# Layer 2's experts in an order by places, and layer 3's attention prepared beside their last two chunks

## What is computed

```python
h = _layernorm(x, axis=-1) * (1 + cb) + sb                      # layer 2
x = x + gb * _L2_ffn_ref(h, ...)
...
h = _layernorm(x, axis=-1) * (1 + ca) + sa                      # layer 3
x = x + ga * _L3_attn_ref(h, W_qkv, b_qkv, W_out, b_out)
h = _layernorm(x, axis=-1) * (1 + cb) + sb
x = x + gb * _L3_ffn_ref(h, ...)

def _L2_ffn_ref(x, ...):
    weights, idx = _gate(xf, gate_w, gate_b)
    combine = (one_hot(idx, E) * weights[..., None]).sum(1)
    h = silu(xf @ We1 + be1) * (xf @ We3 + be3)
    y = einsum('te,ted->td', combine, h @ We2 + be2)
    z = (silu(xf @ ws1 + bs1) * (xf @ ws3 + bs3)) @ ws2 + bs2
    return y + z

def _L3_attn_ref(x, W_qkv, b_qkv, W_out, b_out):
    T, B, D = x.shape
    q, k, v = split(x @ W_qkv + b_qkv)
    scores = einsum('bhqd,bhkd->bhqk', q, k) / sqrt(Dh)
    attn = softmax(where(causal, scores, -inf))
    return (attn @ v) @ W_out + b_out
```

## Time and profile before

| | us |
|---|---|
| median of 3 runs | 3118.23 |
| lowest and highest run | 3110.52 and 3121.22 |
| the profiled execution, device time | 3117.64 |
| its span | 3115.7 |
| PE busy | 2809.0 (90%) |
| DVE busy | 2174.2 (70%) |
| ACT busy | 1692.5 (54%) |
| POOL busy | 1048.9 (34%) |

### The profile page before, as it was taken

One profiled execution on the slowest core, in us unless ns is written; L12 is line 12 of the kernel. 1 busy time (PEld: TensorE's weight loads), 2 busy tenths in 40 slices (PEclk: granted clock), 3 DMA queues, 4 the chain that ended last, 5 costly groups with the idle time before them and its releaser, 6 DMA issues.

```text
span 3115.7 us, 68897 instructions
## 1 busy us (share of the span) xinstructions
PE 2809.0 (90%) x25404; PEld 1878.9 (60%) x25404; DVE 2174.2 (70%) x5846; ACT 1692.5 (54%) x4067; POOL 1048.9 (34%) x1444
## 2 busy tenths in 40 slices
PE   5999999989999999999997998999899889885885
PEld 2566666666666666666665554677666655554664
DVE  5888888855666466666666888556677868864557
ACT  2877777773233377777764666433255442223553
POOL 5877788731000011111113444222433300114323
PEclk8999999999999999999998999999899999897997
DMA  3011111122000011111114443000344422335640
GB/s 101 15 29 29 29 29 29 29 82 84 15 1 1 19 29 29 29 29 29 29 29 138 125 130 109 1 15 1 102 139 121 118 62 56 70 71 151 169 118 28
DMA packets 189836, 188.13 MB, mean 60 GB/s; under 512 B 14288, under 2 KB 166032, under 8 KB 188736
## 3 DMA queue, kind: packets, MB, share of 16 engines
q1 hardware_dynamic: 189504, 183.73, 22.5%
HBM read 130.36 MB, written 53.31 MB: 59 GB/s over the span
## 4 chain that ended last, share of the span: by engine, by line
PE 61%; DVE 21%; issue 6%; ACT 6%; POOL 2%; DMA 2%; SPq 2%; DVEq 0%; POOLq 0%; ACTq 0%
PE pb L174 55%; ACT big L895 4%; PE pb L620 2%; DVE big L2107 2%; DVE big L785 2%; DVE big L240 2%; SPq L1788 2%; DVE big L768 1%; ACT big L171 1%; DVE big L696 1%; DMA big<-parts 1%; DVE big L2579 1%; DVE big L190 1%; DVE big L767 1%; PE pb L553 1%
## 5 line engine op out<-in xcount | busy, mean ns | idle before, releaser
L174 PE MATMUL pb<-big 128*128 128x128 f32 (+13 forms) x20220 | 2528.5, 332 | 186.8 <-DVE big L2107 58.9
L174 PEld LDWEIGHTS pb<-big 128*128 128x128 f32 (+5 forms) x20220 | 1572.0, 146 | 942.5 <-issue 545.8
L171 ACT ACTIVATE big<-pb 128x512 f32<-128x512 f32 (+7 forms) x1444 | 826.1, 619 | 594.6 <-PE pb L174 348.0
L171 ACT ACTIVATE big<-pb,big 128x512 f32<-128x512 f32 (+2 forms) x504 | 308.7, 632 | 677.3 <-PE pb L174 542.1
L2107 DVE TENSOR_REDUCE big<-pb 128x4 f32<-128x1024 f32 (+1 forms) x256 | 278.2, 1087 | 111.6 <-PE pb L174 108.2
L185 POOL TENSOR_TENSOR big<-big 128x128 f32<-128x128 f32 x224 | 99.9, 461 | 748.8 <-DVE big L182 748.8
L895 ACT ACTIVATE big<-big 128x256 f32<-128x256 f32 x512 | 253.9, 497 | 71.0 <-DVE big L790 69.4
L895 ACT ACTIVATE big<-pb,big 128x128 f32<-128x128 f32 (+1 forms) x512 | 255.6, 513 | 64.6 <-DVE big L770 64.1
L974 POOL TENSOR_TENSOR big<-big 128x512 f32<-128x512 f32 x128 | 159.7, 1274 | 247.6 <-DMA big<-recip 247.6
L785 DVE CUSTOM_DVE_ANT_0 big<-pb,big 128x256 f32<-128x256 f32 x512 | 186.6, 421 | 78.4 <-PE pb L174 78.2
L1470 DVE SCALAR_TENSOR_TENSOR big<-pb,big 128x128 f32<-128x128 f32 x512 | 144.0, 344 | 139.1 <-PE pb L174 138.5
(11 more groups left out here) (136 smaller groups left out, 2321.2 us busy)
## 6 DMA issues: line engine op xcount, KB each, us to landing
big<-parts SPq DMA_DIRECT2D x96, 512.0 KB, 4.1
parts<-big SPq DMA_DIRECT2D x384, 96.0 KB, 2.3
big<-recip SPq DMA_DIRECT2D x64, 512.0 KB, 6.7
big<-comb SPq DMA_DIRECT2D x32, 512.0 KB, 8.4
parts<-big SPq DMA_DIRECT2D x192, 64.0 KB, 2.1
big<-gates SPq DMA_DIRECT2D x8, 1024.0 KB, 6.1
big<-in_wa SPq DMA_DIRECT2D x2, 2048.0 KB, 9.0
big<-in_wf SPq DMA_DIRECT2D x1, 3072.0 KB, 14.8
```

The source lines that it names most:

```text
L171: return e.activation(o, i, f, bias=bias, scale=scale)
L174: return e.matmul(o, l, r_, start=start, stop=stop, skip_group_check=True)
```

## The change

- The experts of layer 2 take their tiles by `by_places`: chunk c holds the tiles `8 * (c % 4) + 2 * i + c // 4`, so chunks 0 to 3 are the first half of the places of all batches, and chunks 4 to 7 the second. The modulated copy of a chunk is made by four activations of 128 columns instead of two of 256.
- Layer 3's attention gives a guest of 15 steps, and the experts host it from tick 54 (chunk 6) to tick 68. Steps 0 to 9 hold statistics, norms and turns of its chunks 0 to 3, steps 10 to 14 `qk`, `split` and `v` of groups 0 to 2. SP issues `out` 0, `back` 0, `out` 1, `back` 1 and `out` 2 at the end of the experts' own DMAs; `back` 1 waits until `summed` is 64, that is for the matmuls of tick 63 (`tensor_down`), since its target is memory that the experts still read.
- The fence between the two stages goes. PE waits for the experts' PSUM banks before the loop, and for chunk 7's multiplies at tick 3.
- The gates and weights for the last stage are loaded behind group 6's parts instead of ahead of all.
- Of the eight chunks of results that are added to `X` four, the first half of the places, are transposed and added in ticks 46, 49, 52 and 55 (`y_at`), with banks of the loop's ring; four stay behind the loop.

```diff
@@ -199,14 +199,19 @@
+        def by_places(c):
+            return [8 * (c % 4) + 2 * i + c // 4 for i in range(4)]
         chunks = [0]
...
-            def __init__(self, own_v, own_g, mod, which, slots, r0, two_slots=False, tiles=None):
+            def __init__(self, own_v, own_g, mod, which, slots, r0, two_slots=False, tiles=None, same_order=False):
+                self.ready = (lambda c: 4 * c + 4) if same_order else (lambda c: max(self.tiles(c)) + 1)
                 self.tiles = tiles or (lambda c: range(4 * c, 4 * c + 4))
@@ -222,7 +227,7 @@
                 elif i0 == 0:
-                    e.wait_ge(added, self.r0 - 32 + max(self.tiles(c)) + 1)
+                    e.wait_ge(added, self.r0 - 32 + self.ready(c))
                 stats_vector(e, self.ov, [X[:, self.tiles(c)[i], :] for i in range(i0, i1)], self.slot(c) + i0, mean_made if i1 == 4 else None)
@@ -269,8 +274,10 @@
                 for i, tile in enumerate(self.tiles(c)):
-                    b, d = tile // 2, dst(tile)
-                    src = s.t[:, 128 * i:128 * i + 128].rearrange("p (i t) -> p i t", i=d.shape[1])
+                    b, d = tile // 2, dst(i)
+                    src = s.t[:, 128 * i:128 * i + 128]
+                    if len(d.shape) == 3:
+                        src = src.rearrange("p (i t) -> p i t", i=d.shape[1])
                     t = act(e, d, src, ACT.Identity, self.mod[:, self.which, b:b + 1], self.mod[:, self.which + 1, b:b + 1])
@@ -1186,8 +1193,9 @@
             modulated_at = 3 * nunit + (0, 2, 1)[k]
-            guests_at = 7 * nunit
-            norm = Norm(own, own_g, MODS[k % 2], 2, slots, r0) if X1 is None else None
+            guests_at = (6 if pairs else 7) * nunit
+            tiles = by_places if pairs else lambda c: range(4 * c, 4 * c + 4)
+            norm = Norm(own, own_g, MODS[k % 2], 2, slots, r0, tiles=tiles) if X1 is None else None
@@ -1456,7 +1464,7 @@
                             n = r0 + 4 * c + i
-                            residual_vector(e, n, 4 * c + i, banks[4 + c % 2][:, 128 * i:128 * i + 128], 128).then_inc(gated, 1)
+                            residual_vector(e, n, tiles(c)[i], banks[4 + c % 2][:, 128 * i:128 * i + 128], 128).then_inc(gated, 1)
                     return
...
@@ -1541,7 +1549,9 @@
                         start.ht_free(e)
-                    if p == "turn":
+                    if p == "turn" and pairs:
+                        norm.modulated_tiles(e, c, lambda n: HTS[s][:, 128 * n:128 * n + 128])
+                    elif p == "turn":
                         norm.modulated(e, c, lambda n: HTS[s][:, 256 * n:256 * n + 256])
...
@@ -1699,7 +1709,13 @@
                 guest.ht_free = ht_free
-                guest.mem_free = nothing
+                def mem_free(e):
+                    if pairs:
+                        s = slots["v", 6 * nunit + 7, 0]
+                        e.wait_ge(s.free, s.n)
+                guest.mem_free = mem_free
             yield Stage(tensor, vector, scalar, gpsimd, sync)
@@ -2402,7 +2418,7 @@
             OV = [alloc(512) for _ in range(2)]
-            bqs = alloc(1)
+            bqs = bqs1
             bias_scaled, q_out = sem("bias_scaled3"), sem("q_out3")
@@ -2413,10 +2429,10 @@
             parts = Parts(own_g, p0, 4, wait_qk)
-            ring = BK[5:8]
+            ring = [BK[6], BK[7], BK[5]]
             taken = [0]
             slots = {}
-            norm = Norm(own, own_g, MODS[1], 0, slots, residuals[0], two_slots=True, tiles=lambda c: [8 * (c % 4) + 2 * i + c // 4 for i in range(4)])
+            norm = Norm(own, own_g, MODS[1], 0, slots, residuals[0], two_slots=True, tiles=by_places, same_order=True)
@@ -2427,7 +2443,12 @@
-            prologue = [(g, p) for g in range(3) for p in ("qk", "split", "v") if p != "v" or g < 2]
+            def hosted_step(i):
+                found = [(c, p) for c in range(4) for p, at in (("stats", 0), ("normed", 1), ("ln", 3)) if 2 * c + at == i]
+                return found + {10: [(0, "qk"), (0, "split")], 11: [(0, "v")], 12: [(1, "qk"), (1, "split")], 13: [(1, "v")],
+                                14: [(2, "qk"), (2, "split")]}.get(i, [])
@@ -2438,9 +2459,13 @@
-            def take(*key):
-                slots[key] = ring[taken[0] % 3].use()
+            def take(*key, ring=ring):
+                slots[key] = ring[taken[0] % len(ring)].use()
                 taken[0] += 1
+            def y_at(t):
+                return [(t - 46) // 3] if t >= 46 and (t - 46) % 3 == 0 and (t - 46) // 3 < 4 else []
@@ -2523,13 +2548,26 @@
+            def tensor_hosted(e, i):
+                if i == 0:
+                    e.wait_ge(ld_wi, 48)
+                for g, p in hosted_step(i):
+                    tensor_piece(e, g, p)
+            def tensor_y(e, c):
+                s, v = slots["y", c], slots["c", 16 * (c // 4) + 15]
+                e.wait_ge(v.free, v.n)
+                bk = fill(e, s)
+                for i, ti in enumerate(by_places(c)):
+                    x = e.transpose(bk[:, 128 * i:128 * i + 128], YT[:, ti // 2, 128 * (ti % 2):128 * (ti % 2) + 128], IDF)
+                x.then_inc(s.full, 1)
             def tensor(e):
-                e.wait_ge(ld_wi, 48)
-                for c in range(4):
-                    norm.turn(e, c)
-                for g, p in prologue:
-                    tensor_piece(e, g, p)
+                for bank, n in settled:
+                    e.wait_ge(bank.free, n)
                 for t in range(last):
+                    if t == 3:
+                        e.wait_ge(gated, 96)
                     if t < 64:
@@ -2559,15 +2597,10 @@
                         tensor_piece(e, g, p)
-                s = slots["c", 31]
-                e.wait_ge(s.free, s.n)
-                for c in range(8):
-                    s = slots["y", c]
-                    bk = fill(e, s)
-                    for i in range(4):
-                        ti = 4 * c + i
-                        x = e.transpose(bk[:, 128 * i:128 * i + 128], YT[:, ti // 2, 128 * (ti % 2):128 * (ti % 2) + 128], IDF)
-                    x.then_inc(s.full, 1)
+                    for c in y_at(t):
+                        tensor_y(e, c)
+                for c in range(4, 8):
+                    tensor_y(e, c)
@@ -2614,18 +2647,22 @@
+            def vector_hosted(e, i):
+                if i == 0:
+                    e.wait_ge(ld_wi, 48)
+                    e.tensor_scalar(bqs, bi[:, 0:1], 8.0 ** -0.5, None, ALU.mult).then_inc(bias_scaled, 1)
+                    ones_vector(e)
+                for g, p in hosted_step(i):
+                    vector_piece(e, g, p)
+            def vector_y(e, c):
+                s = slots["y", c]
+                bk = empty(e, s)
+                xs = X[:, 8 * (c % 4):8 * (c % 4) + 8, :].rearrange("p (i h) c -> p i h c", h=2)[:, :, c // 4, :]
+                e.tensor_tensor(xs, xs, bk[:, :].rearrange("p (i c) -> p i c", i=4), ALU.add).then_inc(s.free, 1)
             def vector(e):
-                e.wait_ge(ld_wi, 48)
-                e.tensor_scalar(bqs, bi[:, 0:1], 8.0 ** -0.5, None, ALU.mult).then_inc(bias_scaled, 1)
-                ones_vector(e)
                 pads_vector(e, True)
-                norm.stats(e, 0)
-                for c in range(4):
-                    if c < 3:
-                        norm.stats(e, c + 1)
-                    norm.normed(e, c)
-                for g, p in prologue:
-                    vector_piece(e, g, p)
                 for t in range(last):
...
@@ -2654,12 +2690,14 @@
+            def scalar_hosted(e, i):
+                for g, p in hosted_step(i):
+                    if g == 0 and p == "qk":
+                        start.mem_free(e)
+                        e.wait_ge(bias_scaled, 1)
+                    scalar_piece(e, g, p)
             def scalar(e):
-                for c in range(4):
-                    turned_back(e, c)
-                e.wait_ge(bias_scaled, 1)
-                for g, p in prologue:
-                    scalar_piece(e, g, p)
                 for t in range(last):
...
@@ -2715,23 +2753,29 @@
-            def sync(e):
-                second_gates(e, 3)
-                e.dma_start(WF[:, 0:dr["wf3"].shape[1]], dr["wf3"]).then_inc(ld_wf, 16)
+            def sync_hosted(e):
                 parts.out(e, 0)
...
                 parts.out(e, 1)
-                for g in range(2, 16):
+                e.wait_ge(summed, 64)
+                parts.back(e, 1)
+                parts.out(e, 2)
+            def sync(e):
+                for g in range(3, 16):
                     parts.out(e, g)
                     parts.back(e, g - 1)
+                    if g == 6:
+                        e.wait_ge(gated, 96)
+                        second_gates(e, 3)
+                        e.dma_start(WF[:, 0:dr["wf3"].shape[1]], dr["wf3"]).then_inc(ld_wf, 16)
                 parts.back(e, 15)
-            yield None, None
-            for c in range(4):
-                take("ln", c)
```

(10 more changed lines are left out.)

26 lines of the change are left out of this document (13 added, 13 removed).

## The result

| | before | changed |
|---|---|---|
| median, lowest and highest run, us | 3119.72 (3110.52 to 3124.09, 4 runs) | 3087.56 (3077.55 to 3088.29, 4 runs) |
| the profiled execution, us | 3117.64 | 3088.29 |

The ratio is 0.9893, with a 95% interval of 0.9863 to 0.9924: faster by 1.1%, and 4.6 us over the predicted 3083. Measured a second time beside other kernels, with four runs of it, the ratio was 0.9889 (0.9874 to 0.9904), the median 3084.63. Of `back_at_once`, `back1_behind_out2`, `host_later` and `host_earlier` there is one run each (3086.70, 3084.12, 3091.88 and 3095.59 us), so they are read by marks inside their profiles and not by whole times.

A forecast was written before the change was run, and what follows sets the result against it. TensorE bounds the experts' last chunks, then 37.9 us lie before layer 3's first maximum, with a second hole before tick 4. Summed: -36.0 at tick 8, +0.8 early results, +0.5 gates, -34.7 from 3117.64, so 3083 us; range 3074 to 3099.

The forecast's parts named there:

- order of the places: Experts' chunks of layer 2: four smaller ACT activations a chunk are hidden, cost nothing; 6 us in all without that cover.
- hosted work beside the experts: Experts' chunks 6 and 7: layer 3's hosted preparation makes the experts end 7.5 us later, ends 5 and 12.
- tick 8, hosting included: Layer 3's loop: tick 8's maximum comes 36.0 us earlier, after a new wait of 2.3 us for back 2.
- gates and weights at group 6: Loop at group 6: two SP issues and data sharing the DMA engines cost 0.5 us, ends 0 and 4.
- early results in the loop: Loop ticks 46, 49, 52, 55: four adds cost 3.2 us together, 1.1 each at 46 and 52.
- four adds fewer in the tail: Tail behind the loop: four of DVE's eight transposed chunks leave, 2.4 us less.
- PE work alone: Low end for hosting in chunks 6 and 7: only PE's added turns, qk and v count, 5 us.
- Start of the loop: First score maximum of layer 3: at 2804.9 instead of 2833.40, 28.5 us earlier.
- a granted clock of 1.00 from the experts on through the loop: Sign expected in the changed kernel: PE keeps its full 2.4 GHz clock from the experts on through layer 3's loop.
- Rival A: Loop: the sync queue sets the pace with slow issues, tick 8 some 3 us later, +11 us, 3094; chance 0.15.
- Rival B: Beside the experts: VectorE and GpSimd hold each other up, norms 6.4 us dearer, experts and copies 8 later, 3091; chance 0.10.
- Rival C: Experts' last chunks: PE waits in order for hosted work, 26 us and up to 39, so 3148, slower; chance 0.03.

The follow-up runs named there:

- back_at_once: Changed kernel, but from group 2 on SP issues a group's copies back right behind its own copies out; 3086.70 us, one run.
- back1_behind_out2: Changed kernel with group 2's copies out issued ahead of group 1's copies back, SP's old order for that step; 3084.12 us, one run.
- host_later: Changed kernel with its 15 hosted steps at ticks 57 to 71 instead of 54 to 68; 3091.88 us, one run.
- host_earlier: Changed kernel with its 15 hosted steps at ticks 51 to 65 instead of 54 to 68; 3095.59 us, one run.
- order_alone: Kernel before with only the new order of the places, nothing hosted and no result added sooner; ratio 1.0004 to the kernel before.
- results_in_tail: Changed kernel with all eight results added in the tail, none in the loop; median 3080.06 us, ratio 0.988 to the kernel before.
- again_before: Kernel before, unchanged, run as a second program; ratio 1.0008 to the kernel before.

## Why the prediction was right

By its own steps, against the kernel before. Terms behind chunk 7's add are from the profiled executions of the two kernels.

| step | predicted | measured |
|---|---|---|
| order of the places | 0 | 0 (`order_alone`) |
| hosted work beside the experts | +7.5 | +5.3 |
| tick 8, hosting included | -36.0 | -37.1 |
| ticks 8 to 12 | 0 | +0.9 |
| gates and weights at group 6 | +0.5 | 0 |
| early results in the loop | +3.2 | +4.7 |
| four adds fewer in the tail | -2.4 | -2.4 |
| rest of the tail | 0 | -0.7 (spread) |
| sum | -34.7 | -34.6 |
| ahead of the experts | 0 | +5.3 (spread) |

- **Hosting.** The end I called "PE work alone", 5 (worked out as 5.4), was the answer. The 1.0 for DVE's queue at ticks 54 to 56 and the 1.1 for handshakes weren't there: PE's idle time did not grow. The sign fits: ACT's passes of ticks 57 and 71 start 43.2 us apart, where 44 was forecast and 37.8 was the time before. The measured 5.3 doesn't hang on where the clock's low stretches fall: two profiles of the kernel before have the experts at 210.08 and 206.04, the changed kernel has 215.36, and `results_in_tail`, with the same experts, 211.29.
- **Start of the loop.** The first maximum came 1.39 us after chunk 7's add; I had 1.6. Ticks 0 to 4 took 9.09 us, where I had 8.3, and ticks 4 to 8 13.37, where I had 10.5 and a wait of 2.3. The sign "a granted clock of 1.00 from the experts on through the loop" was wrong: it was 0.81 and 0.93 in the first 42 us, and I had set nothing down for it. The runs show its price for ticks 8 to 9 alone, 1.25 us.
- **SP.** Hole at tick 4 gone, a new one at tick 8: 3.0 us, predicted 2.3. Back 2 was issued 16.5 us after the last add, as worked out, but from there to the maximum it took 7.4 us and not 6.2, 1.0 of it in the two issues. What the prediction did not see is that the first of these is worth nothing (`back1_behind_out2`), and that the second costs 4.3 with what follows.
- **Early results.** The term of the sum that was mis-sized most: 3.2 in the loop measured 4.7. The mechanism was right in part. The wait for the bank is in the trace at tick 52, but not at 46. At tick 52 I took 1.1 and it was 1.96: it and the tick behind it are the loop's fast ones, 2.26 and 1.94 us, in which PE waits for nothing. At 49 and 55 I took 0.5 each and they cost 0.69 and 1.01. The tail's 2.4 came as worked out (DVE's first statistics of the last stage start 17.35 us after tick 63 instead of 19.74). Without them the adds in the tail would have started 0.7 earlier than before, so what they really give is 1.7. The -0.7 of the rest is not the change's: from the last stage's first statistics to the end `before`'s profile takes 72.00 us, `again_before` 71.30 and the changed kernel 71.29.
- **Rival A**: SP did not pace the loop; ticks 8 to 46 take 119.42 us against 118.52 before. **Rival B**: the four hosted norms took 1.12 to 1.25 us, not 2.73, since the hosted splits come after the last of them. The lock is there in small, beside POOL's split of a hosted group. Two of DVE's multiplies L1446 in the changed kernel's chunk 7, and two POOL instructions of the split beside them:
```profile
2798.02 0.70 DVE L1446 TENSOR_TENSOR big<-big 128x512 f32<-128x512 f32 x1 [0.52 <-ACT big L171]
2800.63 1.44 DVE L1446 TENSOR_TENSOR big<-big 128x512 f32<-128x512 f32 x1 [1.12 <-ACT big L171]
```
```profile
2798.26 1.41 POOL L1786 TENSOR_TENSOR big<-big 128x512 f32<-128x512 f32 x1
...
2800.42 1.09 POOL L1790 TENSOR_TENSOR big<-big 128x512 bf16<-128x512 f32 x1
```
The six multiplies of the chunk take 0.90 us in the mean instead of 0.70, 1.2 us in all. The Trainium skill, "SBUF — State Buffer", section "SBUF: two separate sides", would have the other engine blocked fully for a whole instruction. The trace agrees nearly. The POOL instruction of 2800.42 has 0.88 us to go when the multiply of 2800.63 starts, and this one takes 0.75 more than its 0.69. Three others start with 0.23, 0.25 and 0.45 us of a POOL instruction to go and take 0.08, 0.11 and 0.30 more. Where DVE was first, as at 2798.02, POOL pays: 1.41 us instead of 1.09. So the 0.75 of the earlier trace rows by itself said little on the rule, since the side that comes second pays. DVE idles ahead of five of the six multiplies and PE has no gap, so here it was hidden. **Rival C** did not show in the changed kernel, but it is what `host_earlier` is: PE waits 5.4 us ahead of hosted turns, and its clock falls.

The sum agrees to 0.1 us partly by luck: hosting was 2.2 too dear and the gates 0.5, the start of the loop up to tick 8 1.1 too cheap and the early results 1.5, and nothing was set down for the 0.9 behind the wait and the 0.7 of spread. The fence, the hosting and the gates' move were not tried one without the others.

## What to carry to other kernels

When a stage is filled with the next one's preparation, the price is the bounding engine's own added work, as long as the other engines have room in those very ticks: three ticks earlier, where DVE was full, the same steps cost 9.7 us more. Before filling a hole, look for the next thing behind it in the same queue: the hole at tick 4 was free to keep, and the copy back waiting behind another group's copies out cost 4.3, of which 1.3 was PE's clock behind the wait. And work taken out of a tail is not saved where the loop that takes it has no slack: 1.7 us gained, 4.7 paid.
